# Ten groups of constant products issued by TensorE into an unread bank, in a GNN and mixture-of-experts kernel

## The reference

```python
x = x + L0_gnn(layernorm(x), ...)    # relational graph convolution, a gate, a second convolution
x = x + L0_ffn(layernorm(x))         # top 2 of 8 experts and a shared expert
x = x + L1_gnn(layernorm(x), ...)    # graph attention with 12 heads
x = x + L1_ffn(layernorm(x))         # layer norm, causal attention, layer norm, top 2 of 8 experts (capacity 64)
x = x + L2_gnn(layernorm(x), ...)    # two relational graph attentions, ELU between
x = x + L2_ffn(layernorm(x))         # top 1 of 8 experts, capacity 40
x = x + L3_gnn(layernorm(x), ...)    # graph convolution
x = x + L3_ffn(layernorm(x))         # rms norm, attention, rms norm, top 2 of 8 experts, a shared expert
```

## Time and profile before

| | |
|---|---|
| median of three executions | 2093.7 us |
| the profiled execution's own time | 2088.81 us |
| its span, first to last instruction | 2086.7 us |
| TensorE busy | 1905.0 us, 91% of the span |
| VectorE busy | 687.9 us, 33% |
| ScalarE busy | 443.9 us, 21% |
| GpSimd busy | 299.3 us, 14% |
| read from memory | 356.93 MB, 171 GB/s over the span |

### The profile page before, as it was taken

One profiled execution on the slowest core, in us unless ns is written; L12 is line 12 of the kernel. 1 busy time (PEld: TensorE's weight loads), 2 busy tenths in 40 slices (PEclk: granted clock), 3 DMA queues, 4 the chain that ended last, 5 costly groups with the idle time before them and its releaser, 6 DMA issues.

```text
span 2086.7 us, 22016 instructions
## 1 busy us (share of the span) xinstructions
PE 1905.0 (91%) x9548; PEld 1202.0 (58%) x9548; DVE 687.9 (33%) x1209; ACT 443.9 (21%) x815; POOL 299.3 (14%) x173
## 2 busy tenths in 40 slices
PE   7999999999998999988989888878999798999999
PEld 4664445754457888867754333333465444767877
DVE  4316996049983111044231000001412322132110
ACT  0014553045541100033211000000411001121110
POOL 0005885038860000000000000000000000000000
PEclk9999999999999999995999999999999899999999
DMA  9214002230012566530316999999553154113450
GB/s 350 91 34 170 0 1 91 91 140 19 1 66 115 209 248 265 200 155 16 125 57 289 429 428 428 428 428 428 223 201 124 63 224 185 71 66 120 179 202 16
DMA packets 33779, 363.96 MB, mean 174 GB/s; under 512 B 6797, under 2 KB 10133, under 8 KB 11690
## 3 DMA queue, kind: packets, MB, share of 16 engines
q1 hardware_dynamic: 29568, 358.35, 42.9%
q10 hardware_dynamic: 4106, 4.10, 0.7%
HBM read 356.93 MB, written 0.79 MB: 171 GB/s over the span
## 4 chain that ended last, share of the span: by engine, by line
PE 66%; DMA 12%; DVE 11%; POOL 8%; ACT 2%; issue 1%; DVEq 0%; SPq 0%; ACTq 0%
PE banks L111 64%; POOL gate_work L117 8%; DMA weight_ring<-in_L_ffn_c_fc_dram 6%; DVE gate_work L117 5%; DMA weight_ring<-in_L_ffn_c_proj_e_dram 4%; PE banks L114 2%; DVE gate_qiT L131 2%; DMA weight_ring<-in_L_gnn_W_in_dram 1%; DVE stat L247 1%; ACT r_xd L145 0%; DVE xn_tok L122 0%; DMA ident<-in_c_ident_dram 0%; ACT gat_E L145 0%; ACT banks L145 0%; DVE stat L249 0%
## 5 line engine op out<-in xcount | busy, mean ns | idle before, releaser
L117 POOL TENSOR_TENSOR gate_work<-gate_work 128x1024 f32<-128x1024 f32 x144 | 284.4, 1989 | 321.0 <-DVE gate_work L117 317.3
L111 PE MATMUL banks<-gate_sel,gate_rows 96*128 96x512 bf16 x1152 | 279.0, 380 | 28.4 <-DVE gate_work L117 27.9
L111 PE MATMUL banks<-weight_ring,xT 128*128 128x384 f32 x864 | 293.6, 492 | 2.4 <-DVE rgat_xr L134 1.5
L117 DVE TENSOR_TENSOR gate_work<-banks,gate_qT 128x1024 f32<-128x1024 f32 x192 | 226.2, 1220 | 11.0 <-ACT banks L145 1.4
L111 PEld LDWEIGHTS banks<-weight_ring,xT 128*128 128x128 f32 x864 | 162.9, 192 | 111.4 <-issue 11.4
L145 ACT ACTIVATE banks<-banks 128x1024 f32<-128x1024 f32 x192 | 193.3, 1008 | 132.0 <-PE banks L111 132.0
L111 PEld LDWEIGHTS banks<-gate_sel,gate_rows 96*128 96x128 bf16 x1152 | 104.4, 97 | 181.2 <-DVE gate_work L117 74.8
L111 PEld LDWEIGHTS banks<-r_xd,weight_ring 128*128 128x128 f32 x1728 | 197.5, 192 | 9.0 <-issue 1.6
L111 PE MATMUL banks<-r_xd,weight_ring 128*128 128x128 f32 x1728 | 197.9, 275 | 1.2 <-issue 1.2
L117 POOL TENSOR_TENSOR stat<-stat 128x1 f32<-128x1 f32 (+1 forms) x23 | 14.5, 631 | 1246.8 <-DVE stat L121 1111.2
L111 PE MATMUL banks<-xT,weight_ring 128*128 128x256 f32 x792 | 184.9, 386 | 2.4 <-ACT x_tok L148 1.6
(11 more groups left out here) (325 smaller groups left out, 1701.8 us busy)
## 6 DMA issues: line engine op xcount, KB each, us to landing
weight_ring<-in_L_ffn_c_fc_dram SPq DMA_DIRECT2D x32, 2304.0 KB, 23.3
weight_ring<-in_L_ffn_c_proj_e_dram SPq DMA_DIRECT2D x32, 2304.0 KB, 23.3
weight_ring<-in_L_ffn_w_gate_dram SPq DMA_DIRECT2D x8, 2304.0 KB, 12.7
weight_ring<-in_L_ffn_w_up_dram SPq DMA_DIRECT2D x8, 2304.0 KB, 8.7
weight_ring<-in_L_ffn_w_down_dram SPq DMA_DIRECT2D x8, 2304.0 KB, 8.6
weight_ring<-in_L_ffn_w_dram SPq DMA_DIRECT2D x16, 1152.0 KB, 7.6
weight_ring<-in_L_gnn_W_dram SPq DMA_DIRECT2D x7, 2304.0 KB, 13.6
weight_ring<-in_L_gnn_W_rel_dram SPq DMA_DIRECT2D x6, 2304.0 KB, 14.6
```

The costliest lines, as they stand in the source:

```text
L111: return self.e.matmul(out, lhsT, rhs, start=start, stop=stop)
L117: return self.e.tensor_tensor(out, a, b, op)
```

## The change

A helper issues `n` products of `ident` with the first 256 columns of `before` into columns 0 to 255 of a bank (7 unless another is given). No engine reads what they write; the next product into that bank starts a new sum. It is called in ten places, with 5, 5, 20, 8, 6, 10, 3, 10, 8 and 9 products, 84 in all. No wait is added; in `L0_ffn_pe` the wait for the constants moves ahead of the first of them.

```diff
+        def idle_products_pe(pe, n, bank=7):
+
+            for _ in range(n):
+                pe.mm(PS[:, bank, 0:T], ident[:], before[:, 0, :], True, True)

         def L0_ffn_pe(pe):
             (rw, sgb), ready = smalls("L0_ffn")
+            pe.wait_ge(*at("consts"))
+            idle_products_pe(pe, 5)
             tok_to_T_pe(pe, "L0_ffn", "L0_ffn")
             wait_T(pe, "L0_ffn")
             pe.wait_ge(*ready)
-            pe.wait_ge(*at("consts"))
...
             t.then_inc(*mark("gat_vec_ps"))
             pe.wait_ge(*at("gat_vec"))
+            idle_products_pe(pe, 5)
             tok_to_T_pe(pe, "L1_gnn", "L1_gnn")
...
+            idle_products_pe(pe, 20)
             tok_to_T_pe(pe, "L1_ffn_1", "L1_ffn_1")
...
             project_tok_pe(pe, "c_proj", xT, False)
+            idle_products_pe(pe, 8)
             tok_to_T_pe(pe, "L1_ffn_2", "L1_ffn_2")
...
                 pe.wait_ge(*at("gat_vec", ("turned", l, 2)))
+                idle_products_pe(pe, 6)
                 tok_to_T_pe(pe, key, "L2_h")
...
+            idle_products_pe(pe, 10)
             tok_to_T_pe(pe, "L2_ffn", "L2_ffn")
             wait_T(pe, "L2_ffn")
             pe.wait_ge(*ready)
             small_logits_pe(pe, "L2_ffn", xT, sw, NEXP, swb[0:1, :])
+            idle_products_pe(pe, 3, 5)
             for j in (1, 0):
                 pe.wait_ge(*at("diagonal", j))
                 t = pe.mm(PS[:, 6 + j, 0:T], ones[:], wdg[:, j, :], True, True)
             t.then_inc(*mark("route_rows"))
+            idle_products_pe(pe, 10, 5)
             pe.wait_ge(*at("S", "L2_ffn"))
             dispatched_pe(pe, "L2_ffn", wS, wS2, wxd, NEXP * CAP2)
...
+            idle_products_pe(pe, 8)
             tok_to_T_pe(pe, "L3_ffn_1", "L3_ffn_1")
...
             project_tok_pe(pe, "L3o", xT, False)
+            idle_products_pe(pe, 9)
             tok_to_T_pe(pe, "L3_ffn_2", "L3_ffn_2")
```

## The result

The changed kernel took 2076.8 us (median of five runs, 2072.70 to 2080.78), the kernel before beside it 2091.64 us (five runs, 2085.61 to 2094.55). The ratio is 0.9931, 95% interval 0.9908 to 0.9954: 0.7% faster. The forecast of 2085 us was too high by 8 us; "kept everywhere" (2079.5 us) came nearer. The profiled execution took 2077.8 us.

What follows compares the result with a forecast made beforehand. TensorE, 66% of the chain, idles at norms waiting for DVE, then runs at half clock; only the latter can be won. Gains of -10.2 and L1_gnn's +2.0 make -8.2 us: 2085 us from the median, range 2074 to 2098.

Steps and rivals of the forecast that it cites:

- kept everywhere: Rival: every remaining gap is short enough to keep the clock up; -14.2 us, 2079.5 us from the median; chance 0.20.
- The price of a product: Each added 128x128 by 256 float32 product was to take 0.23 us at full clock, 0.41 us at half.
- First norm of L1_ffn, 0: Twenty products take 4.6 of 9.62 us, over 5 us idle remain: gain 0; the other end was -4.5 us.
- Nine groups hidden: All places but L1_gnn: products fit in the wait for DVE directly behind them and cost 0.
- a sign of its being wrong: Wrong if, outside L1_gnn, a group of products ends later than the rows it waits for.
- L1_gnn, +2.0: Five products behind the last wait to end push the transposes back; cold price taken, +2.0 us.
- the slower rival: L1_gnn's delay makes the clock fall behind it: +4.2 us with transposes at half clock, 2094 to 2098 us; chance 0.10.
- Shares of 0.5: Second norm of L1_ffn, L2_ffn, both norms of L3_ffn: half the full clock gain counted, except L2_ffn's gathers, counted whole.
- the fourth rival: L1_gnn's attention, 34.1 us at 0.50: a shift may bring the clock up early, some 8 us; chance 0.05, either way.
- Only after slice 18: Where the half clock lies, read from the profile's slices: not in the long first layer.
- 0, it was up already: L0_ffn: no gain from its five products, since transposes and logits were at full clock.
- The five places counted on for -10.2 us: Second norm of L1_ffn -0.5, L2_h -2.8, L2_ffn -(1.65 + 2.5), L3_ffn's norms -1.15 and -1.6 us.

Runs made afterwards that it cites:

- e8_only_first: The kernel before with only the twenty products of L1_ffn's first norm, the nine other calls removed: 2085.82 us, ratio 0.9980.
- e2_half: The change with every product count halved, 44 products in place of 84: 2083.89 us, ratio 0.9971.
- e1_no_gnn: The change without the five products of L1_gnn, the other 79 kept: 2070.49 us, ratio 0.9908.
- e3_one_row: The change with the same 84 products using one row of the array instead of 128: 2111.12 us, ratio 1.0096.
- e10_joined: The change with L1_gnn's five ahead of the wait, 14 short products in its attention, three ahead of L1_ffn's gather: 2066.81 us, ratio 0.9901.

## Why the prediction was right, and where it failed

- **The price of a product failed, and most of the rest followed from it.** "At full clock twelve products of such a moving shape took 2.75 us, 0.23 us each": the row's x12 counts records, and these were six calls of two records. A product costs 0.46 us at full clock and 0.82 at half. The product count of the change stood beside it, but was never held against a count of calls in the code for the row that gave the price. The Trainium skill, page "FP8 and Floating Point Precision", section "TensorE Precision Notes", has true FP32 as four passes through the array; with the 109 ns for 256 columns that the prediction cites, an estimate of 0.44 us. The trace agrees with it (8.85/20 = 0.44 us in the first norm of L1_ffn). The prediction drew on the 109 ns alone and saw a factor of two where there are four.
- **First norm of L1_ffn, 0.** "Over 5 us of idle remain": 0.94 us remained, for the twenty took 8.85 us. It gained 3.6 us, close to the 4.5 named as the other end. e8_only_first shows it alone; e2_half shows that with 3.33 us left most of it is gone.
- **Nine groups hidden: right for the norms, barely.** With the true price they had 0.35 to 0.94 us to spare, and only as far as the clock was up. In L2_ffn the three ran at half clock for 2.91 us in a wait of 1.75 us, and the diagonals' products followed without idle time; so did the gathers behind the ten (5.31 us against a wait of 4.52). The prediction named this as a sign of its being wrong. Against the operands, which DVE had written at 1654.78 and 1662.02 us, the products came some 0.8 and 0.4 us late.
- **L1_gnn, +2.0: right in mechanism, mis-sized.** The group took 4.08 us behind ACT's copy; the transposes behind it gave 1.3 us back (2.82 to 1.55 us), net +2.6. The prediction had put them at no gain. That delay alone is as large as the slower rival's 4.2, yet the other places gave more than twice that.
- **Shares of 0.5.** The idle time that they were guessed for didn't exist. Transposes were at full clock in every norm, but in all four routers the clock fell in the logits behind them, which the prediction had put down to the idle stretch. L2_ffn therefore gave 2.0 us and not 4.2 (in e1_no_gnn 4.7). L2_h, without logits, gave the 2.8 us of the forecast.
- **The attention** moved by -2.5 us in this pair of profiles with no product in it; that and L3_gnn's -1.6 us are the spread that the fourth rival spoke of, and part of why the profiled -10.9 us isn't the change's own. By the medians, -14.8 us, it is not settled which places gave the other 4 us.
- **Where the half clock lies was misread in L0_ffn.** "Only after slice 18" and "0, it was up already": it was up for the transposes and the logits, but in the kernel before it stood at 0.50 right behind them, from 635.7 to 639.1 and from 642.5 to 649.4 us. A slice is 52 us long and still shows a 9 with 10 us at half clock in it. The five products kept neither fall off (after: 635.0 to 641.8 and 645.2 to 652.1 us).
- **That the sum came near is in part luck.** The five places counted on for -10.2 us gave -7.3 in the profiles. The first norm of L1_ffn, put at 0, gave -3.6, and the other places put at 0 gave -2.6 together; L1_gnn took 2.6. That makes -10.9 beside the -8.2 of the forecast. By the medians, -14.8 us, the forecast saw little more than half of the gain, and "kept everywhere" (-14.2), with a chance of 0.20, had the size.
- **Signs of the profile**: DVE's statistics stayed at 1.02 us a pair; the mean clock, 0.979, lies in the range named (0.973 to 0.98).

## What to carry to other kernels

Before a duration by a count becomes a price, check what the count counts: hold the row's xcount against the calls in the code. In these runs filler ahead of a short dependent step paid where it filled the wait nearly to its end, worked on all rows of the array, and stood ahead of the wait that ends last; half as much gave under half of the gain, and filler behind the last wait pushed the work back by about its full length (4.1 us, of which the faster transposes gave back 1.3). Look also for stretches that run at half clock although the engine is busy, and start the filler before the clock falls there, not in the midst of it.

## What the runs showed of the hardware

- A float32 product 128x128 by 256 columns: two records, 0.46 us at 1.00 and 0.82 to 0.87 us at 0.50; a float32 transpose of 128x128: one record, 0.15 and 0.23 us.
- A busy TensorE was not enough for full clock: products with one row stayed at 0.50 through 17.4 us of back-to-back issue (e3_one_row), where twenty products with 128 rows, begun at 0.50, brought it up (e8_only_first). In the profile after, the clock fell to 0.50 within each router's logits, products with 8 or 9 moving columns.
- An idle stretch of 2.18 us ahead of twelve transposes left the clock up in one norm (1.86 us) and not in another (2.53 us) of one execution (e2_half).
- Six executions of one kernel lay between 2054.7 and 2072.0 us (e10_joined), the fastest with a mean clock of 0.992, the others with 0.983 to 0.986.
